# A transformer block with routed experts on one core: which token tiles shared expert B takes early, where transposed parts are kept, and where late gathers and weighings stand

## What is computed

```
h = layernorm(x) * (1 + ca) + sa
x = x + ga * (tanh(h @ B.T) @ C.T + D * h)
h = layernorm(x) * (1 + cb) + sb
scores = sigmoid(h @ gate_w.T);  idx = top_k(scores + bias, 2);  w = scores[idx] / sum
routed = sum over the two experts e of w * ((silu(h @ W1[e]) * (h @ W3[e])) @ W2[e])
shared = (silu(h @ sw1.T) * (h @ sw3.T)) @ sw2.T      # 704 wide: two experts of 352
x = x + gb * (routed + shared)
```

## Time and profile before

| | |
|---|---|
| median of 3 runs | 570.36 us (569.66 to 571.24) |
| the profiled execution | 571.33 us, its span 569.7 us |
| TensorE matmul (PE) | busy 543.4 us (95%) |
| TensorE weight load (PEld) | 487.3 us (86%) |
| VectorE (DVE) | 286.6 us (50%) |
| ScalarE (ACT) | 176.3 us (31%) |
| GpSimd (POOL) | 263.5 us (46%) |
| DMA | 119.80 MB, mean 210 GB/s |
| chain that ended last | PE 79%, POOL 7%, issue 5%, DMA 4%, DVE 3%, ACT 1% |

### The profile page before, as it was taken

The page is one execution under the profiler, slowest core; times in us unless marked ns, Lnnn a source line. Parts: engine busy times, 40 slices in busy tenths (PEclk is TensorE's granted clock), DMA queues, the critical chain, the costliest instruction groups (busy, mean ns, idle before and its releaser), DMA issues.

```text
span 569.7 us, 11068 instructions
## 1 busy us (share of the span) xinstructions
PE 543.4 (95%) x3129; PEld 487.3 (86%) x3130; DVE 286.6 (50%) x612; ACT 176.3 (31%) x337; POOL 263.5 (46%) x221
## 2 busy tenths in 40 slices
PE   8996899999999995999999999999999999988997
PEld 3665788998999894999999999999999999987896
DVE  3788586686687565442222222222222222158897
ACT  1444345445534330122223222322223223112211
POOL 2599877668666457343016260044443300254630
PEclk9999899999999998999999999999999999999999
DMA  8999266543452889566254946255758313475982
GB/s 309 395 337 382 84 212 249 186 160 116 166 191 106 286 316 375 190 220 227 96 161 157 326 138 231 74 175 192 288 167 310 129 55 110 152 257 188 314 306 79
DMA packets 47915, 119.80 MB, mean 210 GB/s; under 512 B 4752, under 2 KB 5008, under 8 KB 47888
## 3 DMA queue, kind: packets, MB, share of 16 engines
q1 hardware_dynamic: 35088, 67.02, 33.4%
q0 software_dynamic: 12800, 52.43, 26.0%
HBM read 80.38 MB, written 39.06 MB: 210 GB/s over the span
## 4 chain that ended last, share of the span: by engine, by line
PE 79%; POOL 7%; issue 5%; DMA 4%; DVE 3%; ACT 1%; SPq 0%; POOLq 0%; DVEq 0%; ACTq 0%
PE bank L1007 14%; PE bank L1009 14%; PE bank L1008 14%; PE bank L1038 8%; PE bank L1040 7%; PE bank L1039 7%; PE bank L984 4%; PE bank L1045 4%; PE bank L955 2%; PE bank L953 2%; PE bank L954 2%; DMA x_all<-wmod 2%; POOL tmpa L595 1%; DMA xt_low<-xal 1%; POOL x_all L598 1%
## 5 line engine op out<-in xcount | busy, mean ns | idle before, releaser
L1007 PE MATMUL bank<-whi,thi 128*128 (+1 forms) x416 | 139.9, 336 | 8.3 <-issue 8.3
L1008 PE MATMUL bank<-wlo,thi 128*128 (+1 forms) x416 | 135.9, 327 | 0.0
L1009 PE MATMUL bank<-whi,tlo 128*128 (+1 forms) x416 | 135.5, 326 | 0.0
L582 POOL TENSOR_TENSOR wlo<-raw,whi 128x1408 f32 (+3 forms) x24 | 79.6, 3329 | 83.7 <-DMA whi<-w_all 74.0
L1007 PEld LDWEIGHTS bank<-whi,thi 128*128 128x128 f32 x416 | 79.5, 191 | 9.0 <-issue 9.0
L1742 DVE TENSOR_TENSOR gbuf<-s,bank 128x352 f32<-128x352 f32 x52 | 27.0, 520 | 112.5 <-ACT s L927 111.5
L1038 PE MATMUL bank<-whi,gth 128*128 (+1 forms) x201 | 79.9, 397 | 2.3 <-DVE gtl L1305 1.3
L1040 PE MATMUL bank<-whi,gtl 128*128 (+1 forms) x201 | 79.0, 393 | 0.0
L1008 PEld LDWEIGHTS bank<-wlo,thi 128*128 128x128 f32 x416 | 79.0, 190 | 0.0
L1009 PEld LDWEIGHTS bank<-whi,tlo 128*128 128x128 f32 x416 | 78.9, 190 | 0.0
L1039 PE MATMUL bank<-wlo,gth 128*128 (+1 forms) x201 | 78.8, 392 | 0.0
(11 more groups left out here) (222 smaller groups left out, 951.8 us busy)
## 6 DMA issues: line engine op xcount, KB each, us to landing
raw<-w_all POOLq DMA_DIRECT2D x8, 2176.0 KB
whi<-w_all POOLq DMA_DIRECT2D x16, 704.0 KB, 11.5
h<-xs_rows SPq DMA_DIRECT2D x36, 256.0 KB, 2.7
ys_rows<-tmpa SPq DMA_DIRECT2D x36, 256.0 KB, 2.0
x_all<-wmod SPq DMA_DIRECT2D x6, 1024.0 KB, 9.7
whi<-w_all POOLq DMA_DIRECT2D x8, 768.0 KB, 4.6
hs_rows<-h SPq DMA_DIRECT2D x8, 512.0 KB, 5.1
xt_high<-xah SPq DMA_DIRECT2D x8, 512.0 KB
```

The source lines that it names most:

```text
L582: pool.tensor_tensor(wlo[:, bass.ds(off + (SH + a), b - a)], raw[:, a:b], whi[:, bass.ds(off + (SH + a), b - a)].bitcast(F32), ALU.subtrac ...
L1007: pe.matmul(dst, xh[:, j, a], wh, start=(m == 0), stop=False)
L1008: pe.matmul(dst, xh[:, j, a], wl, start=False, stop=False)
L1009: mm = pe.matmul(dst, xl[:, j, a], wh, start=False, stop=(m == KD - 1))
```

## The change

The early tiles of shared expert B are now 12 to 15, the last four (`NC` = 12), and section C takes tiles 0 to 11. The transposed parts of tiles 12 and 13 (pair 6) stay in `xah`/`xal`, and pair 7 is written to `xbh`/`xbl` in place of `xah`/`xal`. So the four early steps read what is on chip: their loads, the two last `store_x` and ScalarE's wait for pair 6's store go. `FIRST_LAST` becomes 12 to 15, then 10 and 11; indices of `x_all`, `wts`, `pos` and `out` follow.

In section C there are four places for transposed parts (`xt_place`: two in `xah`/`xal`, two in `xbh`/`xbl`), each with its own semaphore (`s_xl`). Tiles 0 and 1 are loaded in the routed stage, after the first `store_y`; tiles 2 and 3 where tiles for steps 0 and 1 were loaded; then the load for step k+4 stands where that for k+2 stood. The last step's `gth_b`/`gtl_b` lie in `shi`/`slo`, since `xah` is now in use.

The first early tile's gathers stand one place earlier on GpSimd, so does each after it. `WEIGH_AT` becomes 2, 4, 5, 7, 8, 10, and `weigh` stands behind `gth`. `COMBINE_AT` gives one part to k = 4 and the 18th part moves behind `finish_last(0, 0, 1)`. TensorE's program has section C written out (`steps(..., True)`), where steps 4 to 9 were a loop: 2073 rows where there were 1849.

```
-FIRST_LAST = [*range(NB), *range(NT - NL, NT)]
-WEIGH_AT = [3, 4, 6, 7, 9, 10]
+NC = NT - NB
+FIRST_LAST = [*range(NC, NT), *range(NC - NL, NC)]
+WEIGH_AT = [2, 4, 5, 7, 8, 10]
+COMBINE_AT = [(), (), (), (0, 1), (2,), (3, 4), (5, 6), (7, 8), (9, 10), (11, 12), (13, 14), (15, 16)]
...
-        gth_b, gtl_b = xah[:, 0, 0:FP], xah[:, 1, 0:FP]
+        gth_b, gtl_b = (t[:, :, :].rearrange("p a b -> p (a b)")[:, 0:FP] for t in (shi, slo))
+        xt_place = [(xah, xal, 0), (xah, xal, 1), (xbh, xbl, 0), (xbh, xbl, 1)]
...
-            def load_x(t, j):
-                for dst, src in ((xbh, xth), (xbl, xtl)):
-                    sp.dma_start(dst[:, j, :].bitcast(F32), src[t * P:(t + 1) * P, :]).then_inc(q["C", "xin"][j], 16)
+            def load_x(t):
+                high_, low_, j = xt_place[t % 4]
+                for dst, src in ((high_, xth), (low_, xtl)):
+                    sp.dma_start(dst[:, j, :].bitcast(F32), src[t * P:(t + 1) * P, :]).then_inc(s_xl[t % 4], 16)
...
                 if lo == NP + 2:
-                    sp.wait_ge(s_stp, NP)
-                    sp.wait_ge(s_xts, 32 * (NP - 1))
-                    for t in range(2):
-                        load_x(t, t)
                     sp.wait_ge(s_nat, NP * 16)
...
-                if live(3, lo, hi):
+                if live(3, lo, hi) and lo <= NP:
                     store_x(it - 3)
...
             def next_c(k):
-                if k < NT - NB:
-                    sp.wait_ge(q["S", "up"], iters * 2 + (NB + k - 1))
-                    load_x(NB + k, k % 2)
+                if k < NC:
+                    sp.wait_ge(q["S", "up"], iters * 2 + (NB + k - 3))
+                    load_x(k)
...
-            for t in range(2, NB):
-                sp.wait_ge(q["S", "up"], t - 1)
-                load_x(t, t % 2)
-            sp.wait_ge(s_xts, 32 * NP)
...
             store_y(0, 0)
+            sp.wait_ge(s_xts, 32 * (NP - 2))
+            sp.wait_ge(q["S", "up"], 2)
+            for t in range(2):
+                load_x(t)
...
-                    n = (c - CB - 1) * 2 + j
+                    n = (c - CB - 1) * 2 + j + 1
                     if n < NB + NL:
                         for k in range(2):
                             gather_first(n, k)
...
+                if lo > 3 and not (lo == NP + 1 and p == NP - 1):
                     act.wait_ge(s_xts, p * 32)
-                for j in range(2):
-                    act.activation(xah[:, j, :], h2_bank(lo, j)[:, :], ACT.Copy).then_inc(q["A", "xhi"], 1)
+                dst = xbh if lo == NP + 1 and p == NP - 1 else xah
+                for j in range(2):
+                    act.activation(dst[:, j, :], h2_bank(lo, j)[:, :], ACT.Copy).then_inc(q["A", "xhi"], 1)
...
                 if loaded is not None:
-                    pe.wait_ge(q["C", "xin"][j], loaded * 32)
+                    xh, xl = xt_place[loaded % 4][0:2]
+                    if loaded >= 4:
+                        pe.wait_ge(s_xl[loaded % 4], 32 * (loaded // 4))
+                    else:
+                        pe.wait_ge(q["A", "xlo"], NT)
...
-            iters = steps(pe, step, lambda: pairs_of_b(pe))
+            iters = steps(pe, step, lambda: pairs_of_b(pe), True)
...
-                    for n in range(2 * m, 2 * m + 2):
+                    for n in COMBINE_AT[m + 3]:
                         combine(n // 3, n % 3)
...
                     finish_last(0, 0, 1)
+                    combine(NB + NL - 1, 2)
```

More of the change, by code:

```diff
@@ L247, in build @@
         s_xts = sem("s_xts")
+        s_xl = [sem(f"s_xl{b}") for b in range(4)]
         s_lg = sem("s_lg")
@@ L266, in build @@
                 q[sec, n] = sem(f"{n}_{sec}")
-            q[sec, "xin"] = [sem(f"xin{j}_{sec}") for j in range(2)]
+            if sec == "S":
+                q[sec, "xin"] = [sem(f"xin{j}_{sec}") for j in range(2)]
             q[sec, "ydma"] = [sem(f"ydma{j}_{sec}") for j in range(2)]
@@ L643, in body @@
                     pool.wait_ge(w_ready, 2 * NW)
-                    for t in range(2):
-                        pool.wait_ge(q["C", "xin"][t], 32)
                     fetch_raw(0)
@@ L755, in _ @@
                 gather(CB, j)
+            for k in range(2):
+                gather_first(0, k)
             for c in range(CB + 1, NP - 1):
@@ L928, in step @@
                 k = (c - CB) * 2 + j if sec == "C" else -1
-                if k in WEIGH_AT:
-                    weigh(WEIGH_AT.index(k))
                 act.wait_ge(q["S", "gt"], i * 2 + (j + 1))
@@ L988, in up @@
                 xh, xl = (xah, xal) if sec == "A" else (xbh, xbl)
+                if sec == "A" and isinstance(i, int) and i == NP - 1:
+                    xh, xl = xbh, xbl
                 if loaded is not None:
-                    pe.wait_ge(q["C", "xin"][j], loaded * 32)
+                    xh, xl = xt_place[loaded % 4][0:2]
[3 more added lines that the diff above has]
+                        pe.wait_ge(q["A", "xlo"], NT)
                 elif sec == "A":
@@ L1469, in lows_a @@
             def lows_a(p, lo):
+                high_, low_ = xah, xal
+                if lo == NP + 1 and p == NP - 1:
+                    dve.wait_ge(s_stp, NP)
+                    high_, low_ = xbh, xbl
                 for j in range(2):
                     dve.wait_ge(q["A", "xhi"], p * 2 + (j + 1))
-                    dve.tensor_tensor(xal[:, j, :], h2_bank(lo, j)[:, :], xah[:, j, :].bitcast(F32),
+                    dve.tensor_tensor(low_[:, j, :], h2_bank(lo, j)[:, :], high_[:, j, :].bitcast(F32),
                                       ALU.subtract).then_inc(q["A", "xlo"], 1)
@@ L1711, in finish @@
                     dve.wait_ge(q["C", "ydma"][j], (c - CB) * 16)
-                w = [wts[:, c * 2 + j:c * 2 + j + 1, k] for k in range(2)]
+                w = [wts[:, n - 1:n, k] for k in range(2)]
                 dve.scalar_tensor_tensor(y, tbuf[:, j, :], w[0], bank[5 + j][:, :],
```

25 lines of the change are left out of this document (12 added, 13 removed).

## The result

The changed kernel takes **563.76 us** (median of 7 runs, 563.16 to 567.39), the kernel before 570.36 us on the same chip (568.99 to 572.21); the ratio is 0.9898, with an interval of 0.9868 to 0.9927. It became 6.6 us faster where 13.7 us were forecast, and it lies above the range.

What follows compares the result with a forecast made beforehand. TensorE was taken to bound the long middle, leaving gaps around it to win. Terms -1.3 - 8.7 + 0.5 - 5.3 + 0.5 + 0.6 gave -13.7 us, so 556.7 us; range for 8 in 10: 554.8 to 562.0.

Steps and rivals of the forecast that it cites:

- (a): End of attention stage: pair 7 goes to `xbh`/`xbl`, so TensorE's wait for pair 6's store goes; -1.3 us.
- (b): Shared expert B: early steps read on chip, so TensorE's gap and the slow clock after it go; -8.7 us.
- (c): First gathered tile in B: its rows land just when TensorE comes; +0.5 us, bounds no wait or 6.4 us.
- Rival 1: Step 3 of B: TensorE idles 6.4 us for the first gathered tile, plus slow clock; 564.8 us, chance 0.12 together.
- (d): Middle stage: SP's extra loads of two tiles are covered; cost 0, up to 3 us once if cover is gone.
- (h): Last stage: TensorE's loop written out, 224 rows more; cost 0 for execution.
- (e): Last stage: with four places, loads are used two steps later and the 1.71 us load wait goes.
- (f): Last stage: earlier gathers and later weighing end waits; stretch down to 6.28 us a step, -5.3, late landings +0.5 us.
- Rival 2: Last stage stays late through late gathers, blocked Silu or VectorE; only 1.7 of 5.3 us won, 559.8 us, chance 0.12.
- (g): Tail: the last piece of the sums moves between the last two results, no longer covered by ScalarE; +0.6 us.

Runs made afterwards that it cites:

- e3: The kernel before with only TensorE's loop of the last stage written out; 571.78 us, ratio 0.9996 to the kernel before.
- e15: e11 with the stores of the four on-chip tiles moved out of SP's loop, behind the last step; 559.64 us, ratio 0.9788 to the kernel before.
- e11: e8 with two places for transposed tiles and TensorE's loop kept as a loop; 567.92 us, ratio 0.9952 to the kernel before.
- e12: e8 with each tile's three sums in one step (6 to 11), none left for the tail; 558.31 us, ratio 0.9798 to the kernel before.
- e8: The changed kernel with early gathers behind the fourth to ninth normal ones, weighed in steps 5 to 10, sums later; 558.62 us, ratio 0.9761 to the kernel before.
- e17: e12 unchanged, measured again beside the changed kernel in five rounds; 558.92 us, ratio 0.9775 to the kernel before.
- e5: The changed kernel without the twelve early gathers and the wait for them (output incomplete); 557.61 us, ratio 0.9745 to the kernel before.
- e6: The changed kernel with the same twelve early gathers fetching 16 numbers a row, not 512 (output incomplete); 564.56 us, ratio 0.9871 to the kernel before.
- e9: e8 with the first early pair of gathers moved ahead of the third normal pair; 563.22 us, ratio 0.9890 to the kernel before.
- e14: e9 with its moved pair replaced by two plain DMAs of the same size from GpSimd's queue; 558.65 us, ratio 0.9767 to the kernel before.
- e10: e9 with GpSimd waiting for the first four gathers' rows before the moved pair; 565.86 us, ratio 0.9929 to the kernel before.
- e13: The changed kernel with one more GpSimd wait, for a sum, before each early pair; 562.78 us, ratio 0.9831 to the kernel before.
- e2: The changed kernel with two places for transposed tiles and TensorE's loop kept as a loop; 568.55 us, ratio 0.9930 to the kernel before.
- e18: The changed kernel unchanged, measured and profiled again; 567.06 us, ratio 0.9922 to the kernel before.
- e16: e13 with the first tile weighed one step later and sums begun in step 4; 563.50 us, ratio 0.9885 to the kernel before.
- e1: The changed kernel with early gathers, weighing and sums in the order of before; 564.36 us, ratio 0.9872 to the kernel before.

## Why the prediction was wrong

**(a) and (b) were right, (c) in kind.** I forecast -1.3 - 8.7 + 0.5 = -9.5 us up to the middle; it is -9.38, which is nearer than its parts: -1.64 for the pair at the join, -8.89 for the gap, +1.15 for what came late. The wait at the join is gone; the gap of 6.45 us went with its slow clock; the first gathered tile arrived in time. The half microsecond that I had put ahead of that tile came behind it, and twice: the next two turns are 7.28 and 7.31 us behind the one before, where 6.74 is usual and the first was 6.70 before. Rival 1 named a time of 564.8, nearly the measured one, and is refuted all the same: there is no wait at 223.66. A total that fits is no evidence for a mechanism.

**(d) and (h) held at 0.** The middle has the same length, and e3 prices the written-out loop at nothing.

**(e) held in kind.** No load wait stands in the changed kernel's timeline; e15 prices the four places at 1.0 us (one trace each, not clear of the noise) where I took 1.71. They also shield TensorE from stores that wait in SP's queue, which I had not seen: without that shield the late gathers lose nearly all they won (e11, 9.6 us above e12, measured beside it).

**(f) is the step that failed.** I took the stretch down to 6.28 us a step, -5.3, with +0.5 for late landings; it became 4.16 us longer in the profiled execution, by the estimate above about 2.4 in a middling one. Two things in that step were wrong. I asked of the moved gathers only when their rows land and who waits for them, and bounded the cost by that (0 to 3.6 us). I did not count what the earlier pair does to GpSimd's own queue: it closed the pause behind the fourth gather. And I held all signals to be instant. Rival 2 had the right place, but gave it 559.8 for late rows or a late VectorE, and in the changed kernel neither stands there. With the early gathers behind the fourth to ninth normal ones (e8) the stretch is 75.82 us; my forecast of it was 75.4 + 0.5. The remaining sum was sound: with the gathers so moved, 0.9775 (e17) of 570.36 is 557.5, beside a forecast of 556.7.

**(g)** +0.6 was measured as +0.40 from the turn at 551.96 to the end; undoing it (e12) gives nothing that can be measured.

Shown by runs: that the early gathers make the loss (e5), that the first hole needs no bytes (e6), that one pair of gathers at that place makes it and plain DMAs there do not (e9, e14), and that a pause before the pair takes it away (e10, e13). Not shown: through which part of the chip GpSimd's issuing delays TensorE's signals (or the last writes that they report), whether the length of the run decides or something that mostly comes with it (in e13 signals in a run of eight were on time), and what share of the later, wandering holes is due to the run and what to the bytes.

## What to carry to other kernels

Moving a transfer earlier costs what its issue closes: look at the queue of the engine that issues it, and at whose pauses it fills, before asking when the data lands. Keep GpSimd's gathers in short groups, four at a time here, each behind a wait that is met last, and place consumers by the landing (6 to 8 us here), not by the issue. When an engine starts late on work that the trace shows done, compare the end of the producer with the start of the consumer: a bracket "remote" or "issue" with the producer long done can be a late signal and not a missing operand. See whether another engine that waits for the same work starts late too, and rule out the instruction's other waits first (the 3.26 us "issue" of e13 was a wait for rows, two engines back). And when a run's total matches a rival, check the rival's place in the timeline first.

## What the hardware showed

Late signals of TensorE, by the number of gathers that GpSimd had issued without a pause (under 1.9 us from start to start) when an up product ended, over the twelve steps of the last stage of the 18 traces of the changed kernel and its variants, 210 of 216 up products, those whose semaphore's change the traces hold:

| gathers in the run so far | up products | signal late by |
|---|---|---|
| 0 | 130 | at most 0.7 us |
| 1 to 4 | 62 | at most 1.2 us |
| 5 | 6 | 3.5 to 4.2 us |
| 8 | 12 | 1.1 to 4.1 us, ten of them under 1.6 |

The six of the third row are five third steps (changed kernel, e2, e6, e9, e18) and one at 512.7 us in e16. Without gathers in the run, 0.01 us from the modelled end to the signal is the rule, so the modelled ends can be trusted here.

The up products alone show too little. Counted the same way, the signals of down products and turns are at most 0.02 us late with up to four gathers in the run (but for one of 1.9 us, whose gather began 2.0 us behind the one before it, just over the limit of a run), and with five or more 30 of 49 are over 1.2 us late, the worst by 6.2 to 6.4 us: the down product in the third step of the changed kernel, e2, e6 and e18. The other 19 are not, so the count says when a signal can be late and not when it will be. I had expected signals between engines to take the same small time whatever else runs.

The clock after a hole was not a matter of its length alone: after 3.00, 3.01, 3.14 and 3.19 us (e9, changed kernel, e10, e18) the granted clock stayed full, after 3.13, 3.16 and 3.26 us (e6, e2, e13) it was at its lower level, 1.2 GHz, for part of the next step, which then took 9.04, 7.96 and 7.92 us. Shorter holes had it too: 2.99 us in e1, and 2.25 us in the changed kernel, where the step behind 531.44 took 7.95 us in place of 6.28.
